# Mixture-of-experts stage of a decoder: 32 blocks of 256 rows and 8 of 128 in place of 39 blocks of 256

## The reference

```python
logits = x_flat @ router_w.T; probs = softmax(logits)          # 8 experts
top_v, top_i = jax.lax.top_k(probs, 2); top_v = top_v / sum(top_v)
for k in range(2):                       # C = 1.25 * 4096 / 8 * 2 = 1280 rows an expert
    keep = pos < C                       # pos: how many rows this expert had before
    h = gelu(einsum('ech,ehf->ecf', expert_in, w1))             # 256 -> 1024
    y = einsum('ecf,efh->ech', h, w2)                           # 1024 -> 256
    out = out + y[slot] * (gate * keep)
x = layernorm(x + out)
```

## Time and profile before

| | us |
|---|---|
| median of 3 runs | 2680.21 (2676.41 to 2695.23) |
| the profiled execution | 2689.17 |
| its span, first to last instruction | 2687.4 |
| PE busy | 2370.5 (88%) |
| DVE, ACT, POOL busy | 1349.1, 1136.7, 855.7 |

### The profile page before, as it was taken

How to read it: one execution, slowest core, us unless ns; L and a number is a source line. 1 busy time by engine, 2 the same in 40 slices (tenths; PEclk the granted TensorE clock), 3 DMA queues, 4 the chain that set the end, 5 groups by cost and what they waited for, 6 DMA issues and landing times. The chain is left out here.

```text
span 2687.4 us, 44698 instructions
## 1 busy us (share of the span) xinstructions
PE 2370.5 (88%) x17262; PEld 1822.0 (68%) x17262; DVE 1349.1 (50%) x2497; ACT 1136.7 (42%) x1930; POOL 855.7 (32%) x882
## 2 busy tenths in 40 slices
PE   9688888699997769798998959999996899999994
PEld 4576667466665545564665648888885788888883
DVE  5587778378887760003445436778877111111113
ACT  1466656355565644344233225555653111111113
POOL 2355445144444581000001013445444121222221
PEclk9699999799999989899999979999998899999997
DMA  2343445310110559473121032332331756656634
GB/s 75 84 111 103 116 104 124 102 32 25 43 53 25 190 191 230 119 219 102 32 63 40 16 143 71 110 124 97 99 138 57 273 185 194 181 178 190 193 94 137
DMA packets 214465, 313.24 MB, mean 117 GB/s; under 512 B 63856, under 2 KB 196848, under 8 KB 201072
## 3 DMA queue, kind: packets, MB, share of 16 engines
q1 hardware_dynamic: 191536, 254.47, 31.0%
q0 software_dynamic: 14304, 18.69, 3.9%
q10 hardware_dynamic: 8416, 37.23, 3.6%
HBM read 187.58 MB, written 122.76 MB: 115 GB/s over the span
## 5 line engine op out<-in xcount | busy, mean ns | idle before, releaser
L2605 ACT ACTIVATE me_h<-me_ps_h 128x512 f32<-128x512 f32 x156 | 93.2, 597 | 454.1 <-PE me_ps_h L2585 454.1
L2643 DVE TENSOR_SCALAR me_yo<-me_ps_y,moe_xg 128x256 f32<-128x256 f32 x78 | 37.8, 484 | 476.3 <-PE me_ps_y L2594 428.9
L2533 POOL DMA_INDIRECT xo<-me_yo,me_row x78 | 121.9, 1563 | 441.4 <-DVE me_yo L2643 428.0
L2585 PE MATMUL me_ps_h<-me_xt,me_w 128*128 128x256 f32 x1024 | 226.3, 379 | 0.0
L2594 PE MATMUL me_ps_y<-me_w,me_h 128*128 128x256 f32 x1024 | 226.1, 379 | 0.0
L2594 PEld LDWEIGHTS me_ps_y<-me_w,me_h 128*128 128x128 f32 x1024 | 194.6, 190 | 26.5
L2585 PEld LDWEIGHTS me_ps_h<-me_xt,me_w 128*128 128x128 f32 x1024 | 192.1, 190 | 24.8
L2074 POOL TENSOR_TENSOR l1x_e<-l1x_e,l1x_ri 128x1024 f32<-128x1024 f32 x64 | 121.8, 1903 | 235.3 <-DVE l1x_ri L2358 235.3
L664 POOL TENSOR_TENSOR l0x_e<-l0x_e,l0x_ri 128x1024 f32<-128x1024 f32 x64 | 120.1, 1897 | 201.7 <-DVE l0x_ri L893 201.7
L2193 PE MATMUL l1x_ps_p<-l1x_xct,l1x_w_q 128*128 128x256 f32 x512 | 123.5, 385 | 0.0
L2231 PE MATMUL l1x_ps_o<-l1x_w_o,l1x_ot 128*128 128x256 f32 x512 | 120.4, 389 | 1.4 <-ACT l1x_ot L2304 1.4
(11 more groups left out here) (398 smaller groups left out, 5423.8 us busy)
## 6 DMA issues: line engine op xcount, KB each, us to landing
me_w<-in_w SPq DMA_DIRECT2D x32, 2048.0 KB, 9.7
xs<-dec_zero SPq DMA_DIRECT2D x31, 1032.0 KB, 7.0
k<-kv_kt ACTq DMA_DIRECT2D x16, 1024.0 KB, 6.1
v<-kv_va ACTq DMA_DIRECT2D x16, 1024.0 KB, 5.0
l1x_kt<-k SPq DMA_DIRECT2D x16, 1024.0 KB, 4.9
l1x_va<-v SPq DMA_DIRECT2D x16, 1024.0 KB, 5.7
moe_w_first<-in_w SPq DMA_DIRECT2D x7, 2048.0 KB, 9.9
moe_xg<-xs SPq DMA_DIRECT2D x39, 258.0 KB, 2.8
```

The costliest lines, as they stand in the source:

```text
L2533: pool.indirect_dma_start(token_rows, bass.IndirectOffsetOnAxis(row[:, j % 2, q:q + 1], 0), yo[:, j % 2, q, :], None, compute_op=ALU.add). ...
L2585: last = pe.matmul(ps_h[i % HB][:, f % 2, :], weights(j)[:, FFN * c + f * P:FFN * c + f * P + P], xt[:, j % 2, c, :], start=c == 0, stop=c ...
L2605: act.activation(h[:, j % 2, 2 * i:2 * i + 2, :], ps_h[i % HB][:, :, :], ACT.Gelu).then_inc(gelued, 1)
```

## The change

`PAIRS` = 8192 // 256 = 32 blocks of 256 rows come first, then `SINGLES` = 8 blocks of 128. An expert whose last block holds 1 to 128 rows gives that block to the singles; one whose last block holds more takes a pair. If more than 32 pairs come out (at most 4 more, `EXTRA`), each of the others is worked as two singles. Every step of a block takes its size from `size(j)` (2 halves or 1), and every semaphore threshold is written by `first(j)`, the number of halves before block j. The lists of the pairs are made where both lists were made before; the list of the singles, `lone`, is made by `map_singles` on DVE, inside the experts' stage after the fourth step, and SP waits for it (`singled`) ahead of the loads of block 32. POOL makes four tables for it.

```diff
-                    then(dve.tensor_tensor(over[:, :, :], cnt[:, :].unsqueeze(2).to_broadcast([P, EXPERTS, MAX_GROUPS]),
-                                           levels[:, :, :], ALU.is_gt))
-                    then(dve.tensor_reduce(grp[:, :], over[:, :, :], AX.X, ALU.add))
+                    for half_too in range(2):
+                        then(dve.tensor_tensor(over[:, half_too, :, :], cnt[:, :].unsqueeze(2).to_broadcast([P, EXPERTS, MAX_GROUPS]),
+                                               levels[:, half_too, :, :], ALU.is_gt))
+                    then(dve.tensor_reduce(grp[:, :, :], over[:, :, :, :], AX.X, ALU.add))
+                    dve.tensor_copy(split[:, 0, :], grp[:, 0, :])
+                    then(dve.tensor_tensor(split[:, 1, :], grp[:, 1, :], grp[:, 0, :], ALU.subtract))
+                    for single in range(2):
+                        then(dve.tensor_tensor(sums_[:, single, :, :], split[:, single, :].unsqueeze(1).to_broadcast([P, EXPERTS, EXPERTS]),
+                                               through[:, :, :], ALU.mult))
...
+        def size(j):
+            return Q if j < PAIRS else 1
+
+        def first(j):
+
+            return Q * j if j < PAIRS else Q * PAIRS + j - PAIRS
...
-                    slot_free(pool, added, j, 1, 16 * Q)
-                    for q in range(Q):
-                        item_done(pool, y_gated, Q * j + q)
+                    if j >= 1:
+                        pool.wait_ge(added, 16 * first(j))
+                    for q in range(size(j)):
+                        item_done(pool, y_gated, first(j) + q)
...
+                    else:
+                        b = sp.value_load(lone[0:1, 1, j - PAIRS:j - PAIRS + 1], min_val=0, max_val=Q * PLACES + 1)
+                        sp.dma_start(xg[:, j % XB, 0, :], xs.rearrange("(b p) d -> b p d", p=P)[bass.ds(b, 1), :, :].rearrange("b p d -> (b p) d")
+                                     ).then_inc(xg_loaded[j % XB], 16)
                 for j in range(1, GROUPS):
+                    if j == PAIRS:
+                        sp.wait_ge(singled, SINGLE_STEPS)
                     load_x(j)
                     load_w(j)
...
-                                last = pe.matmul(ps_h[i % HB][:, f % 2, :], weights(j)[:, FFN * c + f * P:FFN * c + f * P + P],
-                                                 xt[:, j % 2, c, :], start=c == 0, stop=c == 1)
+                                last = pe.matmul(ps_h[i % HB][:, f % 2, 0:P * size(j)], weights(j)[:, FFN * c + f * P:FFN * c + f * P + P],
+                                                 xt[:, j % 2, c, 0:P * size(j)], start=c == 0, stop=c == 1)
...
-                    for q in range(Q):
-                        slot_free(pe, y_gated, Q * j + q, Q)
+                    for q in range(size(j)):
+                        if j >= 1:
+                            pe.wait_ge(y_gated, first(j - 1) + min(q + 1, size(j - 1)))
...
-                        act.activation(h[:, j % 2, 2 * i:2 * i + 2, :], ps_h[i % HB][:, :, :], ACT.Gelu).then_inc(gelued, 1)
+                        act.activation(h[:, j % 2, 2 * i:2 * i + 2, 0:P * size(j)], ps_h[i % HB][:, :, 0:P * size(j)], ACT.Gelu).then_inc(gelued, 1)
...
+                def map_singles():
...
+                    dve.wait_ge(consts, 4)
+                    dve.scalar_tensor_tensor(out=site[:, :], in0=split[:, 0, :], scalar=float(Q), in1=units[:, :], op0=ALU.mult, op1=ALU.add)
+                    then(dve.tensor_tensor(begun[:, :], split[:, 3, :], split[:, 1, :], ALU.subtract))
+                    then(dve.tensor_tensor(own[:, :, :], back[:, :, :], each(begun[:, :]), ALU.is_ge))
+                    then(dve.tensor_tensor(own2[:, :, :], back[:, :, :], each(split[:, 3, :]), ALU.is_lt))
...
-                unrolled(GROUPS, [(0, copy_xt), (2, rows_of), (2, gate_y)])
+                unrolled(GROUPS, [(0, copy_xt), (2, rows_of), (2, gate_y), (3, lambda j: map_singles() if j == 0 else None)])
...
-GROUPS = (TOPK * B * S - EXPERTS) // GROUP + EXPERTS
+SINGLES, EXTRA = EXPERTS, EXPERTS // 2
+PAIRS = TOPK * B * S // GROUP
+GROUPS = PAIRS + SINGLES
...
-PLACES = EXPERTS * MAX_GROUPS + GROUPS - TOPK * B * S // GROUP - 1
+PLACES = EXPERTS * MAX_GROUPS + EXTRA
```

More of the change, by code:

```diff
@@ L1988, in l1_xattn @@
         number = kit.sb("number", [P, TILES])
[L1989 to L1993, removed]
+        cnt = kit.sb("cnt", [P, EXPERTS])
+        sums_ = kit.sb("sums", [P, 2, EXPERTS, EXPERTS])
+        over = kit.sb("over", [P, 2, EXPERTS, MAX_GROUPS])
+        grp = kit.sb("grp", [P, 2, EXPERTS])
+        ended = kit.sb("ended", [P, PAIRS + EXTRA, EXPERTS])
+        at_, past, spot = (kit.sb(n, [P, PAIRS + EXTRA]) for n in ("at", "past", "spot"))
         ps_s = kit.ps("ps_s", [P, 2, 4, P])
@@ L2456, in map_groups @@
+                    dve.tensor_scalar(extra[:, 0, :], at_[:, PAIRS:], float(EXPERTS - 1), None, ALU.min)
+                    then(dve.tensor_tensor(ended[:, :, :], ended[:, :, :], over_groups(split[:, 0, :]), ALU.mult))
                     then(dve.tensor_reduce(past[:, :], ended[:, :, :], AX.X, ALU.add))
@@ L2486, in moe_experts @@
         acc = kit.sb("acc", [P, TILES, D])
+        back = kit.sb("back", [P, SINGLES, EXPERTS])
+        units, order = kit.sb("units", [P, EXPERTS]), kit.sb("order", [P, EXPERTS])
+        half = kit.sb("half", [P, EXTRA, 2])
+        begun, site = kit.sb("begun", [P, EXPERTS]), kit.sb("site", [P, EXPERTS])
+        own, own2 = kit.sb("own", [P, SINGLES, EXPERTS]), kit.sb("own2", [P, SINGLES, EXPERTS])
+        found = kit.sb("found", [P, 4, SINGLES])
+        other = kit.sb("other", [P, 2, EXTRA, 2])
+        lone = kit.sb("lone", [P, 2, SINGLES], I32)
         pad = kit.sb("pad", [P, 2, Q])
@@ L2641, in gate_y, with then, each @@
[L2641 to L2642 removed]
+                    if j >= 2:
+                        dve.wait_ge(added, 16 * first(j - 1))
+                    for q in range(size(j)):
+                        item_done(dve, down, first(j) + q)
                         dve.tensor_scalar(yo[:, j % 2, q, :], ps_y[q][:, 0:D], xg[:, j % XB, q, D:D + 1], None, ALU.mult).then_inc(y_gated, 1)
+                def map_singles():
+                    done = [0]
+                    def then(ins):
+                        ins.then_inc(singled, 1)
+                        done[0] += 1
+                        dve.wait_ge(singled, done[0])
+                    def each(a):
+                        return a.unsqueeze(1).to_broadcast([P, SINGLES, EXPERTS])
+                    dve.wait_ge(consts, 4)
[3 more added lines that the diff above has]
+                    then(dve.tensor_tensor(own2[:, :, :], back[:, :, :], each(split[:, 3, :]), ALU.is_lt))
+                    then(dve.tensor_tensor(own[:, :, :], own[:, :, :], own2[:, :, :], ALU.mult))
+                    then(dve.tensor_reduce(found[:, 0, :], own[:, :, :], AX.X, ALU.add))
+                    then(dve.tensor_tensor(own2[:, :, :], own[:, :, :], each(order[:, :]), ALU.mult))
+                    then(dve.tensor_reduce(found[:, 1, :], own2[:, :, :], AX.X, ALU.add))
+                    then(dve.tensor_tensor(own2[:, :, :], own[:, :, :], each(site[:, :]), ALU.mult))
+                    then(dve.tensor_reduce(found[:, 2, :], own2[:, :, :], AX.X, ALU.add))
+                    then(dve.tensor_scalar(found[:, 3, :], found[:, 0, :], -1.0, 1.0, ALU.mult, ALU.add))
+                    dve.tensor_tensor(other[:, 0, :, :], extra[:, 0, :].unsqueeze(2).to_broadcast([P, EXTRA, 2]),
+                                      found[:, 3, :].rearrange("p (a b) -> p a b", b=2), ALU.mult)
+                    then(dve.scalar_tensor_tensor(out=other[:, 1, :, :], in0=extra[:, 1, :].unsqueeze(2).to_broadcast([P, EXTRA, 2]),
+                                                  scalar=float(Q), in1=half[:, :, :], op0=ALU.mult, op1=ALU.add))
+                    then(dve.tensor_tensor(other[:, 1, :, :], other[:, 1, :, :], found[:, 3, :].rearrange("p (a b) -> p a b", b=2), ALU.mult))
+                    then(dve.tensor_tensor(lone[:, :, :], other[:, :, :, :].rearrange("p k a b -> p k (a b)"), found[:, 1:3, :], ALU.add))
+                    assert done[0] == SINGLE_STEPS
```

84 lines of the change are left out of this document (52 added, 32 removed).

## The result

| | before | after |
|---|---|---|
| median of the timed runs, us | 2678.31 (4 runs, 2676.32 to 2695.23) | 2644.25 (4 runs, 2640.64 to 2648.78) |
| ratio to before, 95% interval | | 0.986 (0.9816 to 0.9904) |
| ratio in the five rounds of a second session | | 0.9846 (0.9819 to 0.9873) |
| span of the profiled execution, us | 2687.4 | 2640.2 |
| first transposes of the experts' stage to the first reading back of the result, us | 565.5 | 525.6 |

The kernel is 1.4 to 1.5% faster. The forecast was 2639.4 us, 40.8 us less. The first comparison gave 34.1 us less between medians, the second, with 15 runs of before, 0.0154 x 2691.74 = 41.5 us. The last row of the table is the one to go by: it is free of what earlier stages do, and says 39.9.

The account below looks back on a forecast made before the run. PE's passes alone were taken to bound the experts' stage: 99.8 us removed, 57.7 added, 42.1 saved, less 1.3 for the tail, gives 40.8 us less, 2680.2 to 2639.4 us; the range for 8 in 10 was 2628 to 2655.

Parts of the forecast that it names:

- The bound: Experts' stage: PE busy for 512.70 of 512.70 us, others wait for it; a 256-row block takes 14.255 us, seven 99.8.
- A single: One 128-row block on PE: transposes 0.22, `up` 3.54, `down_` 3.455, together 7.2 us; eight cost 57.7 us.
- the interval of L1862: Float32 passes of 128 columns in another stage, 0.111 us each; taken as the price of a single's `up`, 3.54 us.
- that of L1918: Dearer 128-column passes in another stage, 0.118 us each with waits for DVE between; `up` 3.79 us, 40.1 us saved.
- The tail: Last two singles: PE waits 0.7 us for one accumulator, last add 0.6 us further behind PE; +1.3 us.
- The rival in its expectation: Rival stated for the run with both accumulators: both tail waits add up, so the stage takes 524.6 us; no chance given.
- The covers of the map: Start of experts' stage: 1.4 us longer map within 2.9 us of cover; 3.1 us singles' list in DVE's idle time; cost 0.
- The loads: Weight loads of 9.7 us run five blocks ahead; the last three singles' land over 10 us early; cost 0.
- the rival that hung on it (8 x 9.7 us): Weight loads become the singles' bound, 9.7 us each, 77.6 for eight; 20.9 us saved, 2659 us; chance 4%.
- `up` at full price: Weight load sets a pass, so a single's `up` stays 6.91 us; 13.8 us saved, 2666 us; chance 5%.
- The granted clock: Singles run at PE's lower clock, 14.4 us each; 16.6 us lost, 2697 us; chance 3%.
- The upper end of the range, 41.5: Most microseconds saved in the forecast's own range, 38.8 to 41.5, before the scatter of medians.

Follow-up runs that it names:

- before_32: The kernel before with its last 7 blocks of 256 rows left out; experts' stage 465.7 us against 565.5, timed ratio to before 0.9612.
- up_wide: The changed kernel with `up` of a single moving 256 columns in place of 128; experts' stage 552.1 us against 525.6, timed ratio to before 0.9931.
- singles_mid: The changed kernel with the eight singles at steps 16 to 23, pairs behind them; experts' stage 523.8 us against 525.6, timed ratio to before 0.9849.
- two_acc: The changed kernel with the singles using both `down_` accumulators in turn; experts' stage 525.6 us, the same as the changed kernel; not timed beyond its trace.
- many_singles: The changed kernel with 24 pairs and 24 singles, some rows worked three times, others not at all; experts' stage 527.4 us against 525.6.
- wb3_after: The changed kernel with 3 buffers of weights in place of 6; experts' stage 539.1 us against 525.6.

## Why the prediction was right, and where its steps were off

- **The bound.** That the stage is PE's passes and nothing else held before and after; the removed part was 99.8 us to the digit (before_32).
- **A single: 7.2 us forecast, 7.24 measured.** `up` took 3.57, 0.112 us a pass: the interval of L1862, not that of L1918, whose longer one has waits in it. up_wide shows the step behind it, that the price is the columns.
- **The tail: 1.3 us forecast, 1.5 measured.** The rows of the changed kernel give 0.9 for PE's wait and 0.6 for the last add, and singles_mid gives 1.5 back. The two terms may be added, since the second is counted from PE's end, which the first has already put off; the prediction's own times, the last add at 5.7 us after the end of down(38), came out as 5.79 (2603.36 - 2597.57). But they have one cause, the add of 38, and the prediction names two: without PE's wait the last add would have been as late. two_acc took the wait away and nothing moved. The rival in its expectation, 0.7 us less, doesn't follow from the prediction's times.
- **The covers of the map.** 1.5 us left and 0 cost, as forecast; measured 1.56.
- **The loads.** "Land one after the other at T + 10, T + 20 and T + 30" was wrong in its mechanism, and with it the price of the rival that hung on it (8 x 9.7 us): many_singles kept 7.25 us a single without a gap of PE. What made singles wait was loads issued too late, in wb3_after, and there it was the rows that PE waited for, a load that the prediction counted by its size alone. The conclusion, no cost with six buffers, held.
- **The rivals.** `up` at full price would have given 13 us, and up_wide shows that price and that it isn't paid. The granted clock stayed at 1.00 through the singles, which had no wait of PE before the last; wb3_after shows it fall where PE waits. That the passes are short did nothing to it, in many_singles for 165 us.
- **The sum.** 40.8 us forecast; 39.9 in the stage, 40.3 without its start, 41 in the second session's medians. The terms as measured close on the 40.3: 99.8 - 8 x 7.245 - 1.5. The upper end of the range, 41.5, is worked out nowhere in the prediction, and PE's last pass, forecast 41.5 us earlier, came 40.4 earlier within the stage. The first session's 34 is within its interval (26 to 49 us); the first attention stage alone varied by 24 us over the thirteen profiles.

The rule of the Trainium skill that I had set against the change (TensorE: Matmul & The Clock Gate, Part 3, "What overlaps and what doesn't") has weight loads overlap running matmuls only where they aim at another row group. These runs disagree for full-array float32 passes: 0.112 us for a weight load and 128 columns, 0.216 for the same weight load and 256.

## What to carry to other kernels

When padding comes from rounding up to a tile, half tiles can take part of it away: here the seven blocks beyond the 32 cost 99.8 us, and the eight half ones 59.9, 40% less. A half tile costs half as long as each pass is paid by its moving columns: look for a pass of the narrow form anywhere in the trace before counting on it. Small blocks stand better in the middle than at the end, where nothing covers the adds (1.5 us by the traces, too little for the timed runs). Count the waits at a tail as one chain, since the one that ends last hides the others. And compare kernels by the stage that changed: here it repeats to 0.4 us while the whole moves by tens.

## What the runs showed of the hardware

- Loads of 2 MB that each took 9.4 us from issue to landing in the median (7.7 at the least) followed at 7.25 us, 19 in a row, at 320 GB/s with the rows (many_singles): more than one was under way at a time.
- The 129 KB loads that SP issued just behind one of 2 MB landed 7.7 to 9.9 us after their issue (wb3_after); in the changed kernel, with more time between, they took 2.0 to 4.3.
- The same stage of the same instructions took 403 to 427 us with PE's granted clock over it at 0.96 to 0.90, from one execution to the next.
- After waits of PE of 2.72 and 2.50 us its granted clock was 0.50 and 0.66 in the next 2 to 3 us, after one of 3.45 us it was 1.00 (wb3_after).
